# Cross attention of the first chain: values from undivided exponentials, sums by a matrix of ones, division behind the values

## The chip, the core and the metric

The kernel runs on one core of one Trainium2 chip. The metric is the device time of one execution in microseconds (us), the median of several runs. The core has a matrix engine (TensorE, PE in the profile, with PEld for its weight loads), VectorE (DVE), ScalarE (ACT), GpSimd (POOL) and the queue that issues DMAs (SP). Each engine works through its own instructions in program order and waits on semaphores for the others.

## What is computed

The reference passes x (2 x 1024 x 256, fp32) and a context of 2 x 64 rows through four layers: a decoder block (L0), a gated routing update (L1), a transformer block (L2) and a last cross attention (L3). The change touches the cross attention of L0 alone, with H = 16 heads of 16 dimensions and S = 64 context rows:

```python
q = (h @ q_w + q_b).reshape(B, T, H, HD).transpose(0, 2, 1, 3)
k = (enc @ k_w + k_b).reshape(B, S, H, HD).transpose(0, 2, 1, 3)
v = (enc @ v_w + v_b).reshape(B, S, H, HD).transpose(0, 2, 1, 3)
attn = jnp.einsum('bhtd,bhsd->bhts', q, k) * scale
attn = jnp.where(enc_mask[:, None, None, :], neg, attn)
attn = jax.nn.softmax(attn, axis=-1)
ca = jnp.einsum('bhts,bhsd->bhtd', attn, v).transpose(0, 2, 1, 3).reshape(B, T, C)
x = x + ca @ out_w + out_b
```

## The kernel before

The program is a row of parts. The one of interest is `part_chain0`, which carries everything of L0 behind its self attention, and all of L1. It takes the tokens in 4 blocks (`BLOCKS`). A block holds two streams s = 0 and 1, one for each batch entry, and a stream has two tiles t = 0 and 1 of 128 tokens. Block 0 and block 3 are written out; blocks 1 and 2 are turns of one loop (`chain_blocks`). Each stream owns four of the eight banks of PSUM, `ch.ps[s]`, 128 x 2048 fp32, and every stage of the block writes there in turn, so a stage has to be read out before the next may write.

Every engine has its order of work written out by hand in `emit`. For the cross attention of a block before:

- PE makes the scores of both streams: 1024 columns for a tile, 16 heads of 64 context rows (L1117, with the mask added by L876).
- DVE takes for each of the four pairs (s, t) in turn the maximum of each head (L987) and the difference (L989, which writes `ch.scores`). ACT takes the exponential of a pair in place (L1009). DVE sums the exponentials of a pair per head (L976) and inverts the 16 sums (L979), each pair's sums standing behind the difference of the next pair. POOL multiplies the pair's 1024 columns by the inverses (L1023).
- PE then runs `turn(0)`, `values(0)`, `turn(1)`, `projected(0)`, `values(1)`, `projected(1)`. `turn(s)` transposes 16 tiles of 128 x 128 into all four banks of the stream (L1136). `values(s)` multiplies by the values (L1143): 8 matmuls whose weights are only 32 columns wide (`e.vcol`, two heads of 16 dimensions), so that four of them stand side by side in the array; they write `ch.ps[s][:, 0:512]`. `projected(s)` multiplies by the output weights (L1152) and adds the bias (L876).
- Between `turn` and `values` the transposed tile goes to SBUF as `ch.pT[s]`: ACT copies stream 0 (L1012), DVE copies stream 1 in one instruction of 128 x 2048 (L996). Between `values` and `projected` ACT copies the result to `caT[s]` (L1342).
- Behind its copy of stream 1 DVE has `finish_block(i - 1)` in its queue, except in block 0. This is the norm n6 that closes the block before, with names in `c_t_` (L806, L811, L839, L846), and two answers of POOL that it waits for (L827, L830). Only then come, for each stream, the sum with x (L1031) and the norm n3, whose result `c_h` PE turns (L883) before the MLP begins (L1217).

A fp32 matmul stands as two rows in the trace and as one in the lists of instructions below.

Of the kernel before, what the change touches and what calls it, by code (L numbers as in the profile page):

```python
# [5 lines left out]
ALU = mybir.AluOpType  # L6
ACT = mybir.ActivationFunctionType
# [586 lines left out]
def part_context0(nc, e, A, later):  # L594
    with ExitStack() as ctx:
# [55 lines left out]
        @block.vector  # L651
        def _(dve):
            dve.memset(e.vcol[:], 0.0).then_inc(zeroed, 1)
            dve.wait_ge(w_in, ALL_W)
            for b in range(B):
                dve.tensor_scalar(e.bias0[:, b], mask8[:, b].unsqueeze(1).to_broadcast([P, 8, S2]), MASKED, None,
                                  ALU.mult)
            dve.tensor_scalar(e.q_bs[:], q_b[:], 0.25, None, ALU.mult)
            dve.wait_ge(gp.sem, gp.value("second"))
            head_rep = head16[:].unsqueeze(2).to_broadcast([P, 8, S2])  # L660
            dve.wait_ge(ev.sem, ev.value("kT"))
            for b in range(B):
                for g in range(KC):
                    rep = kT[:, g, b * S2:(b + 1) * S2].unsqueeze(1).to_broadcast([P, 8, S2])
                    dve.tensor_tensor(out=e.kbd[:, b, g].rearrange("p (h s) -> p h s", s=S2), in0=rep, in1=head_rep,
                                      op=ALU.mult)
            dve.wait_ge(zeroed, 1)
            dve.wait_ge(pe.sem, pe.value("v"))
            by_head = lambda ap: ap.rearrange("p (c e d) -> p c e d", c=8, e=2)
            for b in range(B):  # L670
                for x in range(2):
                    rows = slice(S2 * x, S2 * x + S2)
                    dve.tensor_tensor(out=e.vcol[rows, b, :, 16 * x:16 * x + 16],
                                      in0=by_head(ps["v"][rows, b * C:(b + 1) * C])[:, :, x, :],
                                      in1=by_head(v_brep[rows])[:, :, x, :], op=ALU.add)
# [57 lines left out]
def norm_steps(name):  # L733
    return [f"{name}.stats", f"{name}.moments", f"{name}.h"]
# [225 lines left out]
    return ch.scores[s][:].rearrange("p t n -> p (t n)")[:, 0:2 * cols].rearrange("p (t n) -> p t n", t=2)  # L960


def cross_vector_steps(name):
    return [f"{name}.{x}" for x in ("top0", "less0", "top1", "less1", "total0", "inverse0", "total1", "inverse1",
                                    "turned_kept")]


def cross_vector(dve, ch, name, i, cols):

    heads = cols // S2  # L970
    by_head = lambda ap: ap.rearrange("p (h k) -> p h k", k=S2)
# [11 lines left out]
    for s in range(B):  # L983
        for t in range(2):
            src, top = by_head(ch.ps[s][:, t * cols:(t + 1) * cols]), ch.top[s][:, t, 0:heads]
            after(dve, ch.te[s], f"{name}.scores{t}", i)
            dve.tensor_reduce(top, src, AX.X, ALU.max).then_inc(ch.dve[s].sem, ch.dve[s].one(f"{name}.top{t}"))  # L987
            after(dve, ch.dve[s], f"{name}.top{t}", i)
            dve.tensor_tensor(out=sc(s, t), in0=src, in1=top.unsqueeze(2).to_broadcast([P, heads, S2]),  # L989
                              op=ALU.subtract).then_inc(ch.dve[s].sem, ch.dve[s].one(f"{name}.less{t}"))  # L990
            if last:
                sums(*last)
            last = (s, t)
    sums(*last)
    after(dve, ch.te[1], f"{name}.turned", i)
    dve.tensor_copy(ch.pT[1][:, 0:cols // P, :].rearrange("p c n -> p (c n)"), ch.ps[1][:, 0:2 * cols]).then_inc(  # L996
        ch.dve[1].sem, ch.dve[1].one(f"{name}.turned_kept"))
# [67 lines left out]
def part_chain0(nc, e, A):  # L1065
    with ExitStack() as ctx:
        w = e.w0
        te_steps = ["n2.T", "ca.q", "ca.scores0", "ca.scores1", "ca.turned", "ca.v", "ca.out", "n3.T", "mlp.up", "mlp.down", "n4.T", "rt.scores",
                    "rt.turned", "rt.routed", "n5.T", "gates", "cand"]
        dve_steps = (norm_steps("n2") + cross_vector_steps("ca") + ["ca.x"] + norm_steps("n3")  # L1070
                     + ["xc"] + norm_steps("n4") + ["rt.top", "rt.minus", "rt.inverse", "rt.probs"]
                     + norm_steps("n5") + ["reset"])
        act_steps = ["n2.hT", "ca.qT", *cross_scalar_steps("ca"), "ca.vT", "n3.hT", "mlp.gelu",
                     "x.T", "n4.hT", "rt.exp", "rt.kept", "n5.hT",
                     "r", "u", "tanh"]
        ch = Chain(nc, ctx, "c0", te_steps, dve_steps, act_steps,
                   ["n2.shifted", "n2.rstd", "ca.probs0", "ca.probs1", "n3.shifted", "n3.rstd", "n4.shifted",
                    "n4.rstd", "n5.shifted", "n5.rstd"], e.biases0.shape[1])
        tail = Tail(nc, ctx, ch, "c0_tail", norm_steps("n6") + ["out.x"],
                    ["cand.less", "cand.gated", "mixed", "n6.shifted", "n6.rstd"])  # L1080
# [1 line left out]
        ROWS_MADE = 1 + 5 * (e.biases0.shape[1] // PIECE)  # L1082
        stT, inT, rT = ch.sb("stT", [P, KC, 256]), ch.sb("inT", [P, KC, 256]), ch.sb("rT", [P, KC, 256])
        qT, caT = ch.sb("qT", [P, KC, 256]), ch.sb("caT", [P, KC, 256])
        u, cand = ch.sb("u", [P, 2, C]), ch.sb("cand", [P, 2, C])
        rp, rpT = ch.sb("rp", [P, 2, P]), ch.sb("rpT", [S2, 256])
        top, total = ch.sb("rtop", [P, 2]), ch.sb("rtotal", [P, 2])
# [11 lines left out]
        def _(te):  # L1099
# [31 lines left out]
            def cross(i):  # L1131
                def turn(s):
                    for t in range(2):
                        after(te, ch.pool[s], f"ca.probs{t}", i)
                        for c in range(8):
                            ins = te.transpose(ch.ps[s][:, c * 256 + t * P:c * 256 + (t + 1) * P],  # L1136
                                               ch.scores[s][:, t, c * P:(c + 1) * P], e.ident[:])
                    ins.then_inc(ch.te[s].sem, ch.te[s].one("ca.turned"))

                def values(s):  # L1140
                    after(te, (ch.act, ch.dve)[s][s], "ca.turned_kept", i)
                    for c in range(8):
                        ins = te.matmul(ch.ps[s][32 * (c % 4):32 * (c % 4) + 32, 256 * (c // 4):256 * (c // 4 + 1)],  # L1143
                                        e.vcol[:, s, c, :], ch.pT[s][:, c, :], start=True, stop=True)
                    ins.then_inc(ch.te[s].sem, ch.te[s].one("ca.v"))

                def projected(s):
                    after(te, ch.act[s], "ca.vT", i)
                    for t in range(2):
                        dst = ch.ps[s][:, 512 + t * C:512 + (t + 1) * C]  # L1150
                        for g in range(KC):
# [111 lines left out]
        def _(dve):  # L1263
# [14 lines left out]
            def emit(i, first, last):  # L1278
                one = lambda s, name: (ch.dve[s].sem, ch.dve[s].one(name))
                x = lambda s: tokens(e, s, i)  # L1280
                if first:
                    head(0)
                    assert bias_rows(dve, ch, e.biases0, PIECE) == ROWS_MADE
                cross_vector(dve, ch, "ca", i, 1024)
                if not first:
                    finish_block(i - 1)
                for s in range(B):
# [34 lines left out]
        def _(act):  # L1322
# [13 lines left out]
            def emit(i, first, last):  # L1336
                if first:
                    head(0)
                cross_scalar(act, ch, "ca", i, 1024)
                for s in range(B):  # L1340
                    after(act, ch.te[s], "ca.v", i)
                    act.activation(caT[s][:].rearrange("p g t -> p (g t)"), ch.ps[s][:, 0:512],  # L1342
                                   ACT.Identity).then_inc(*one(s, "ca.vT"))
                for s in range(B):
                    after(act, ch.te[s], "n3.T", i)
                    turned_scalar(act, ch, s, 0, ch.hT[s], w.vec["ln3_g"], w.vec["ln3_b"]).then_inc(*one(s, "n3.hT"))
# [50 lines left out]
        def _(pool):  # L1397
# [3 lines left out]
            def emit(i, first, last):  # L1401
                if first:
                    norm_gpsimd(pool, ch, e, "n2", 0)
                cross_gpsimd(pool, ch, "ca", i, 1024)
                if not first:
                    norm_gpsimd(pool, tail, e, "n6", i - 1)
                for name in ("n3", "n4", "n5"):
# [887 lines left out]
def program(nc, A, out):  # L2295
    with ExitStack() as ctx:
# [27 lines left out]
        front = ctx.enter_context(ExitStack())  # L2324
        fb = lambda n, s, d=F32: front.enter_context(nc.sbuf_tensor(n, s, d))
        e.kbd, e.vcol = fb("kbd", [P, B, KC, 512]), fb("vcol", [P, B, 8, 32])
        e.q_w, e.q_bs, e.o_w = fb("q_w", [P, KC, C]), fb("q_bs", [P, KC]), fb("o_w", [P, KC, C])

        e.biases0 = fb("biases0", [P, 4 * C + B * 512])
# [36 lines left out]
```

## Time and profile before

| | us |
|---|---|
| median of 3 runs | 2385.2 (2384.72 to 2385.51) |
| the profiled execution | 2383.92 |
| its span, first to last instruction | 2382.2 |
| `part_chain0` in it | about 419, from 457 to 876 |
| mean granted clock of TensorE | 0.943 of full speed |

The span is what the profiler shows; the device time of the same execution is 1.7 us longer. Over the span PE is busy 88%, DVE 47%, ACT 39%, POOL 33%. Within `part_chain0` a block takes 103 to 107 us. The profile also gives the clock that the throttle granted to TensorE: 1.00 stands for 2.4 GHz and 0.50 for 1.2 GHz.

### The profile page before, as it was taken

What the parts mean: (1) busy time and instruction counts of PE and PEld (TensorE: products, weight loads), DVE (VectorE), ACT (ScalarE), POOL (GpSimd) and SP (SyncE); (2) the same over time, 40 slices, a digit from 0 to 9 for tenths busy, and PEclk for the clock granted to TensorE, in tenths of its full rate; (3) what the DMA queues carried; (4) which work ended last, traced back from release to release, by engine and by line L of the source; (5) the groups of instructions that cost most, each with busy time, mean ns of one, the idle gap of its engine ahead of it and who ended that gap; (6) DMA issues with size and microseconds to landing.
All of it is one profiled execution on the core that took longest, in us unless ns stands there. A gap on an engine that the chain in (4) does not pass through costs nothing. (4 is left out here: it accounts for less than half of the span.)

```text
span 2382.2 us, 27289 instructions
## 1 busy us (share of the span) xinstructions
PE 2086.4 (88%) x10510; PEld 1203.7 (51%) x10550; DVE 1130.7 (47%) x2031; ACT 933.0 (39%) x1435; POOL 777.5 (33%) x508
## 2 busy tenths in 40 slices
PE   2789998487979767999999999999998979898987
PEld 1444444275757554433343335334433857576766
DVE  5476672435252435455535554555450152525343
ACT  2256665133333322555545553554454422121211
POOL 3211100013032121566646664666466010202011
PEclk8899999699989887999999999999999989899989
DMA  5723320400000004000000000000000500000000
GB/s 121 130 37 44 42 29 2 113 1 0 1 0 0 1 1 122 1 1 1 1 1 1 1 1 1 1 2 1 1 2 1 161 27 1 9 1 9 0 9 9
DMA packets 48266, 52.77 MB, mean 22 GB/s; under 512 B 14730, under 2 KB 39052, under 8 KB 47732
## 3 DMA queue, kind: packets, MB, share of 16 engines
q1 hardware_dynamic: 48148, 51.17, 10.3%
q8 instruction: 77, 1.26, 0.2%
q14 instruction: 41, 0.34, 0.1%
HBM read 41.31 MB, written 8.80 MB: 21 GB/s over the span
## 5 line engine op out<-in xcount | busy, mean ns | idle before, releaser
L1731 POOL TENSOR_TENSOR total<-total,pr 128x1024 f32<-128x1024 f32 x192 | 465.1, 2423 | 241.9 <-ACT pr L1872 229.0
L1872 ACT ACTIVATE pr<-sc 128x1024 f32<-128x1024 f32 x256 | 260.0, 1022 | 355.3 <-PE sc L1651 355.3
L1752 DVE TENSOR_REDUCE pmax<-ring 128x1 f32<-128x512 f32 x512 | 325.9, 685 | 133.9 <-PE ring L1618 125.8
L1669 PE MATMUL o<-pr,v_pair 128*64 128x512 f32 x1024 | 275.7, 617 | 1.2
L1651 PE MATMUL sc<-q_full,k_full 64*128 64x512 f32 x1024 | 267.2, 591 | 0.0
L522 ACT ACTIVATE probs<-s 128x512 f32<-128x512 f32 (+1 forms) x304 | 163.2, 575 | 101.5 <-PE s L309 55.0
L1618 PE MATMUL ring<-k_round,q_round 64*128 64x512 f32 x512 | 185.0, 598 | 5.3 <-DVE pmax L1752 4.3
L1023 POOL TENSOR_TENSOR c_scores<-c_scores,c_total 128x1024 f32<-128x1024 f32 (+1 forms) x48 | 77.0, 1616 | 344.5 <-DVE c_total L979 344.5
L1618 PEld LDWEIGHTS ring<-k_round,q_round 64*128 64x128 f32 x512 | 74.4, 188 | 155.1 <-DVE pmax L1752 97.2
L394 DVE TENSOR_REDUCE row_max<-s 128x1 f32<-128x640 f32 (+3 forms) x128 | 127.3, 1020 | 47.3 <-PE s L291 47.1
L1669 PEld LDWEIGHTS o<-pr,v_pair 128*64 128x64 f32 x1024 | 51.2, 134 | 144.4 <-issue 142.6
L1731 POOL TENSOR_TENSOR total<-pr 128x1024 f32<-128x1024 f32 x32 | 75.3, 2353 | 141.8 <-ACT pr L1872 141.8
L2166 PE MATMUL c_ps<-c_hT,hT 128*128 128x256 f32 x512 | 117.3, 392 | 4.4 <-ACT c_hT L898 4.4
L288 PE MATMUL s<-k_stack,q_stack 128*128 128x512 bf16 (+3 forms) x367 | 92.9, 328 | 30.3 <-DMA k_stack<-mask_dram 16.7
L898 ACT ACTIVATE c_hT<-c_ps,c_ln_b,c_ln_g 128x256 f32<-128x256 f32 x64 | 32.4, 561 | 213.2 <-PE c_ps L883 213.2
L948 PE MATMUL c_ps<-vw,c_pT 128*128 128x256 f32 x384 | 100.0, 421 | 13.3 <-ACT c_pT L1012 13.3
L2166 PEld LDWEIGHTS c_ps<-c_hT,hT 128*128 128x128 f32 x512 | 100.2, 197 | 19.7 <-ACT c_hT L898 5.4
L1648 PE MATMUL sc<-shift,picks 64*128 64x512 bf16 x512 | 104.8, 387 | 4.8 <-DMA shift<-top_dram 4.8
L827 POOL TENSOR_TENSOR c_rstd<-c_moments,eps 128x2 f32<-128x2 f32 x48 | 9.4, 196 | 304.2 <-DVE c_moments L811 304.2
L1651 PEld LDWEIGHTS sc<-q_full,k_full 64*128 64x128 f32 x1024 | 104.6, 192 | 6.9
L306 PE MATMUL s<-q_stack,k_stack 128*128 128x512 bf16 (+3 forms) x361 | 99.3, 325 | 1.2 <-ACT probs L522 0.9
L948 PEld LDWEIGHTS c_ps<-vw,c_pT 128*128 128x128 f32 x384 | 79.8, 213 | 28.4 <-ACT c_pT L1012 15.3
(285 smaller groups left out, 3430.1 us busy)
## 6 DMA issues: line engine op xcount, KB each, us to landing
qk_dram<-qk_parts SPq DMA_DIRECT2D x32, 192.0 KB, 3.1
q_stack<-qk_dram SPq DMA_DIRECT2D x48, 128.0 KB
k_stack<-qk_dram SPq DMA_DIRECT2D x48, 128.0 KB
x<-in_x SPq DMA_DIRECT2D x4, 512.0 KB, 7.3
mlp_w<-in_L_xattn_mlp_w SPq DMA_DIRECT2D x2, 1024.0 KB, 8.1
wq<-in_L_xattn_Wq SPq DMA_DIRECT2D x2, 1024.0 KB, 6.6
wo<-in_L_xattn_Wo SPq DMA_DIRECT2D x2, 1024.0 KB, 14.9
hT<-in_L_xattn_ff_w SPq DMA_DIRECT2D x1, 2048.0 KB, 19.0
```

The costliest lines, as they stand in the source:

```text
L306: ins = te.matmul(dst[:, x * width:(x + 1) * width], k[:, j, kt * P:(kt + 1) * P], q[:, j, c0:c0 + width], start=True, stop=not diagonal)
L394: dve.tensor_reduce(row_max[:, heads[0], t:t + 1], src[:, 0:(t + 1) * P], AX.X, ALU.max).then_inc(s1_free, 1)
L522: act.activation(probs[at % KEPT][:, heads[0]:heads[-1] + 1, 0:width], s2[u % RING][:, 0:len(heads) * width].rearrange("p (j q) -> p j q", ...
L948: ins = te.matmul(dst, ch.pT[s][:, c, t * P:(t + 1) * P], vw[:, s, c, :], start=c == 0, stop=c == cols // P - 1 and out_bias is None)
L1618: te.matmul(ring[i % RING][:], qr[head[j], t * P:(t + 1) * P], kr[head[j], halves[half]], start=True, stop=True).then_inc(s1_made, 1)
L1648: te.matmul(s2[at % 2][:, j], picks[head[j]], shift[n % 2][head[j], halves[half]], start=True, stop=False)
L1651: ins = te.matmul(s2[at % 2][:, j], kf[n % 2][head[j], keys], qf[n % 2][head[j], halves[half]], start=False, stop=True)
L1669: ins = te.matmul(o[64 * j:64 * j + 64], v[n % 2][:, kt, 64 * j:64 * j + 64], probs[(U * n + u) % KEPT][:, j], start=kt == 0, stop=kt == T ...
L1731: pool.tensor_tensor(out=total[half][:], in0=other[:], in1=probs[at % KEPT][:], op=ALU.add).then_inc(sums, 1)
L1752: dve.tensor_reduce(part_max[:, j, t, half:half + 1], ring[i % RING][:], AX.X, ALU.max).then_inc(s1_free, 1)
L1872: act.activation(probs[here % KEPT][:], s2[at % 2][:], ACT.Exp).then_inc(s2_free, 1)
L2166: ins = te.matmul(ch.ps[s][:, 1024 * part + 256 * f:1024 * part + 256 * (f + 1)], w.f1[:, k, chunk * P:(chunk + 1) * P], ch.hT[s][:, k, :] ...
```

## The change

Only the cross attention of `part_chain0` changes; the two later cross attentions, which share helpers with it, keep their sums.

```diff
@@ setup, VectorE @@
             dve.memset(e.vcol[:], 0.0).then_inc(zeroed, 1)
+            dve.memset(e.sums_of[:], 0.0).then_inc(zeroed, 1)
+            dve.wait_ge(zeroed, 2)
+            for x in range(2):
+                dve.memset(e.sums_of[S2 * x:S2 * x + S2, 16 * x:16 * x + 16], 1.0)
...
-            dve.wait_ge(zeroed, 1)
@@ cross_vector @@
-            if last:
+            if last and sums_made:
                 sums(*last)
             last = (s, t)
-    sums(*last)
+    if sums_made:
+        sums(*last)
@@ part_chain0, TensorE, cross @@
                     for t in range(2):
-                        after(te, ch.pool[s], f"ca.probs{t}", i)
+                        after(te, ch.dve[s], "ca.less1", i)
+                        after(te, ch.act[s], f"ca.exp{t}", i)
...
                         ins = te.matmul(ch.ps[s][32 * (c % 4):32 * (c % 4) + 32, 256 * (c // 4):256 * (c // 4 + 1)],
                                         e.vcol[:, s, c, :], ch.pT[s][:, c, :], start=True, stop=True)
+                    for c in range(8):
+                        ins = te.matmul(ch.ps[s][32 * (c % 4):32 * (c % 4) + 32, 1024 + 256 * (c // 4):1280 + 256 * (c // 4)],
+                                        e.sums_of[:], ch.pT[s][:, c, :], start=True, stop=True)
                     ins.then_inc(ch.te[s].sem, ch.te[s].one("ca.v"))
 
                 def projected(s):
-                    after(te, ch.act[s], "ca.vT", i)
+                    after(te, ch.dve[s], "ca.vT", i)
@@ part_chain0, VectorE, emit @@
-                cross_vector(dve, ch, "ca", i, 1024)
+                cross_vector(dve, ch, "ca", i, 1024, sums_made=False)
+                for s in range(B):
+                    after(dve, ch.te[s], "ca.v", i)
+                    dve.reciprocal(inverse[s][:], ch.ps[s][:, 1024:1536]).then_inc(*one(s, "ca.inverse"))
+                    after(dve, ch.dve[s], "ca.inverse", i)
+                    dve.tensor_tensor(out=caT[s][:].rearrange("p g t -> p (g t)"), in0=ch.ps[s][:, 0:512],
+                                      in1=inverse[s][:], op=ALU.mult).then_inc(*one(s, "ca.vT"))
                 if not first:
                     finish_block(i - 1)
@@ part_chain0, ScalarE, emit @@
-                for s in range(B):
-                    after(act, ch.te[s], "ca.v", i)
-                    act.activation(caT[s][:].rearrange("p g t -> p (g t)"), ch.ps[s][:, 0:512],
-                                   ACT.Identity).then_inc(*one(s, "ca.vT"))
@@ part_chain0, GpSimd, emit @@
-                cross_gpsimd(pool, ch, "ca", i, 1024)
```

`e.sums_of` is a 128 x 32 matrix with ones where a row and a column belong to the same head of a pair. A matmul with it gives the sum of the head's exponentials, 16 times over, at the places where the values of that head lie; so the division is one by one between two 128 x 512 arrays.

Two places in the order of instructions of block 3, the written out one (blocks 0 to 2 have the same order). First TensorE, from the transposes of stream 0 to the first projection of stream 1, before:

```order
L1136 MATMUL c0_ps0<-ident,c0_scores0 128x128 x16
L1143 MATMUL c0_ps0<-c0_pT0,vcol 32x256 x8
L1136 MATMUL c0_ps1<-ident,c0_scores1 128x128 x16
L1152 MATMUL c0_ps0<-o_w,c0_caT0 128x256 x2
L876 MATMUL c0_ps0<-c0_rows,c0_ones 128x256
L1152 MATMUL c0_ps0<-o_w,c0_caT0 128x256 x2
L876 MATMUL c0_ps0<-c0_rows,c0_ones 128x256
L1143 MATMUL c0_ps1<-c0_pT1,vcol 32x256 x8
L1152 MATMUL c0_ps1<-o_w,c0_caT1 128x256 x2
```

and with the change, where lines are numbered a little higher:

```order
L1145 MATMUL c0_ps0<-ident,c0_scores0 128x128 x16
L1152 MATMUL c0_ps0<-c0_pT0,vcol 32x256 x8
L1156 MATMUL c0_ps0<-c0_pT0,sums_of 32x256 x8
L1145 MATMUL c0_ps1<-ident,c0_scores1 128x128 x16
L1165 MATMUL c0_ps0<-o_w,c0_caT0 128x256 x2
L879 MATMUL c0_ps0<-c0_rows,c0_ones 128x256
L1165 MATMUL c0_ps0<-o_w,c0_caT0 128x256 x2
L879 MATMUL c0_ps0<-c0_rows,c0_ones 128x256
L1152 MATMUL c0_ps1<-c0_pT1,vcol 32x256 x8
L1156 MATMUL c0_ps1<-c0_pT1,sums_of 32x256 x8
L1165 MATMUL c0_ps1<-o_w,c0_caT1 128x256 x2
```

The groups keep their order; eight matmuls with `sums_of` have come behind each stream's values.

Then VectorE with the change, from the last difference of the cross attention to the start of `finish_block` (names in `c0_t_`). Before, L996 stood directly ahead of the rows of `finish_block`:

```order
L994 TENSOR_TENSOR c0_scores1<-c0_ps1,c0_top1 128x1024
L1002 COPY c0_pT1<-c0_ps1 128x2048
L1300 RECIPROCAL c0_inverse0<-c0_ps0 128x512
L1302 TENSOR_TENSOR c0_caT0<-c0_ps0,c0_inverse0 128x512
L1300 RECIPROCAL c0_inverse1<-c0_ps1 128x512
L1302 TENSOR_TENSOR c0_caT1<-c0_ps1,c0_inverse1 128x512
L794 MEMSET c0_t_spare0 1x1
L809 BN_STATS c0_t_stats0<-c0_xc0 128x6 x2
```

The two divisions stand between the copy of stream 1 and `finish_block`, and both streams' `caT` come from this queue.

## Rows read from the trace of the kernel before

**Rows 1.** Busy time, `part_chain0`: stretch, length, five engines with counts, clock, DMA

```profile
457.00:876.00 419.00, 352.34 (x1700) 271.38 (x1698) 172.43 (x414) 137.62 (x275) 87.82 (x109) 0.91 0.00 1
```

**Rows 2.** Timeline, block 1, softmax: start, length, engine, line, work [idle before it]

```profile
564.86 1.23 DVE L987 TENSOR_REDUCE c_top<-c_ps 128x16 f32<-128x1024 f32 x1 [6.79 <-PE c_ps L876]
566.12 1.23 DVE L989 TENSOR_TENSOR c_scores<-c_ps,c_top 128x1024 f32<-128x1024 f32 x1
...
568.51 1.23 DVE L989 TENSOR_TENSOR c_scores<-c_ps,c_top 128x1024 f32<-128x1024 f32 x1
...
570.91 0.38 PE L876 MATMUL c_ps<-c_rows,c_ones 96*128 96x512 bf16 x1
...
577.27 1.06 ACT L1009 ACTIVATE c_scores<-c_scores 128x1024 f32<-128x1024 f32 x1 [2.69 <-DVE c_scores L989]
...
578.73 3.76 POOL L1023 TENSOR_TENSOR c_scores<-c_scores,c_total 128x1024 f32<-128x1024 f32 x2 [1.85 <-DVE c_total L979]
578.94 1.94 ACT L1012 ACTIVATE c_pT<-c_ps 128x1024 f32<-128x1024 f32 x2 [0.61 <-PE c_ps L1136]
```

**Rows 3.** Timeline of block 1, values and projections, and what follows

```profile
580.93 1.93 PE L1143 MATMUL c_ps<-c_pT,vcol 128*32 128x256 f32 x16 [2.03 <-ACT c_pT L1012]
...
582.80 2.44 PE L1136 MATMUL c_ps<-ident,c_scores 128*128 128x128 f32 x16
...
584.96 0.73 PEld L1152 LDWEIGHTS c_ps<-o_w,c_caT 128*128 128x128 f32 x4
...
585.27 2.29 DVE L996 COPY c_pT<-c_ps 128x2048 f32<-128x2048 f32 x1 [5.25 <-PE c_ps L1136]
...
586.91 0.27 PE L876 MATMUL c_ps<-c_rows,c_ones 96*128 96x256 bf16 x1
587.49 0.42 DVE L806 BATCH_NORM_STATS2 c_t_stats<-c_xc 128x6 f32<-128x256 f32 x1
...
587.62 1.07 PE L1143 MATMUL c_ps<-c_pT,vcol 128*32 128x256 f32 x16 [0.43 <-DVE c_pT L996]
...
593.63 0.69 DVE L1031 TENSOR_TENSOR x<-c_ps,x 128x512 f32 x1
...
597.27 1.11 PE L883 MATMUL c_ps<-ident,c_h 128*128 128x128 f32 x4 [5.65 <-DVE c_h L818]
...
599.50 6.07 PE L1217 MATMUL c_ps<-c_hT,mlp_w 128*128 128x256 f32 x16 [1.11 <-ACT c_hT L898]
```

**Rows 4.** VectorE's groups by shape, whole program: count, busy us, mean ns, idle before

```profile
L979 DVE RECIPROCAL c_total<-c_total 128x16 f32<-128x16 f32 x32 | 8.1, 253 | 1.1
...
L979 DVE RECIPROCAL c_total<-c_total 128x8 f32<-128x8 f32 x16 | 3.3, 203 | 0.6
...
L1302 DVE RECIPROCAL c_rtotal<-c_rtotal 128x2 f32<-128x2 f32 x8 | 1.3, 166 | 6.1 <-ACT c_rp L1363 6.1
```

**Rows 5.** Busy time by stretches of 4 us, columns as in rows 1

```profile
573.00:577.00 4.00, 1.71 (x9) 1.31 (x10) 3.93 (x5) 1.06 (x1) 2.03 (x2) 0.57 0.00 0
...
581.00:585.00 4.00, 4.00 (x32) 2.73 (x33) 0.00 (x0) 0.60 (x1) 1.49 (x1) 0.65 0.00 0
...
593.00:597.00 4.00, 0.00 (x0) 0.00 (x0) 2.83 (x11) 0.00 (x0) 0.89 (x2) 0.63 0.00 0
...
601.00:605.00 4.00, 4.00 (x13) 3.23 (x12) 0.00 (x0) 0.00 (x0) 0.00 (x0) 0.59 0.00 0
...
705.00:709.00 4.00, 4.00 (x10) 3.19 (x11) 0.74 (x2) 0.00 (x0) 0.35 (x1) 0.50 0.00 0
...
713.00:717.00 4.00, 4.00 (x20) 3.54 (x19) 0.00 (x0) 2.87 (x7) 0.00 (x0) 1.00 0.00 0
```

**Rows 6.** Timeline of block 0: start of the softmax, sum with x, turning of n3

```profile
467.77 1.23 DVE L987 TENSOR_REDUCE c_top<-c_ps 128x16 f32<-128x1024 f32 x1 [0.70 <-PE c_ps L876]
...
491.13 0.68 DVE L1031 TENSOR_TENSOR x<-c_ps,x 128x512 f32<-128x512 f32 x1
...
495.11 0.60 PE L883 MATMUL c_ps<-ident,c_h 128*128 128x128 f32 x4
```

More of the change, by code:

```diff
@@ L960, in scores_of, with cross_vector_steps, cross_vector @@
     return ch.scores[s][:].rearrange("p t n -> p (t n)")[:, 0:2 * cols].rearrange("p (t n) -> p t n", t=2)
-def cross_vector_steps(name):
+def cross_vector_steps(name, sums=True):
+    if not sums:
+        return [f"{name}.{x}" for x in ("top0", "less0", "top1", "less1", "turned_kept")]
     return [f"{name}.{x}" for x in ("top0", "less0", "top1", "less1", "total0", "inverse0", "total1", "inverse1",
                                     "turned_kept")]
-def cross_vector(dve, ch, name, i, cols):
+def cross_vector(dve, ch, name, i, cols, sums_made=True):
     heads = cols // S2
@@ L1069, in part_chain0 @@
                     "rt.turned", "rt.routed", "n5.T", "gates", "cand"]
-        dve_steps = (norm_steps("n2") + cross_vector_steps("ca") + ["ca.x"] + norm_steps("n3")
+        dve_steps = (norm_steps("n2") + cross_vector_steps("ca", False) + ["ca.inverse", "ca.vT", "ca.x"] + norm_steps("n3")
                      + ["xc"] + norm_steps("n4") + ["rt.top", "rt.minus", "rt.inverse", "rt.probs"]
                      + norm_steps("n5") + ["reset"])
-        act_steps = ["n2.hT", "ca.qT", *cross_scalar_steps("ca"), "ca.vT", "n3.hT", "mlp.gelu",
+        act_steps = ["n2.hT", "ca.qT", *cross_scalar_steps("ca"), "n3.hT", "mlp.gelu",
                      "x.T", "n4.hT", "rt.exp", "rt.kept", "n5.hT",
@@ L1076, in part_chain0 @@
         ch = Chain(nc, ctx, "c0", te_steps, dve_steps, act_steps,
-                   ["n2.shifted", "n2.rstd", "ca.probs0", "ca.probs1", "n3.shifted", "n3.rstd", "n4.shifted",
+                   ["n2.shifted", "n2.rstd", "n3.shifted", "n3.rstd", "n4.shifted",
                     "n4.rstd", "n5.shifted", "n5.rstd"], e.biases0.shape[1])
@@ L1084, in part_chain0 @@
         qT, caT = ch.sb("qT", [P, KC, 256]), ch.sb("caT", [P, KC, 256])
+        inverse = ch.sb("inverse", [P, 512])
         u, cand = ch.sb("u", [P, 2, C]), ch.sb("cand", [P, 2, C])
@@ L2326, in program @@
         e.kbd, e.vcol = fb("kbd", [P, B, KC, 512]), fb("vcol", [P, B, 8, 32])
+        e.sums_of = fb("sums_of", [P, 32])
         e.q_w, e.q_bs, e.o_w = fb("q_w", [P, KC, C]), fb("q_bs", [P, KC]), fb("o_w", [P, KC, C])
```

## The prediction

> **What bounds the kernel now.** I read the busy shares of the page first: PE is busy 88% of the span, so time is lost where PE stands still or runs at the low clock. The stretches then show that the chain which is changed takes 419 us and that PE is busy in 352 of them [rows 1]. The timeline of one block shows where the other 67 us lie: in each of the four blocks PE waits during the softmax of the cross attention, and again between the last projection and the turning of n3. So the cross attention is a path of dependent steps on several engines, not work that PE covers, and a step moved on that path counts in full.
>
> The path of block 1. DVE starts at 564.86 and goes through maximum, difference, sums and reciprocal of four pairs. The last exponential starts at 577.27, POOL's last two products end at 582.49, while ACT copies the transposed stream 0 from 578.94 to 580.88 [rows 2]. PE makes values(0) from 580.93 and turn(1) from 582.80 to 585.24; DVE copies stream 1, and has this behind it at 587.49, when `finish_block` starts; that takes 6.14 us, up to the sum with x at 593.63 [rows 3]. Everything later (norm n3, its turning at 597.27, the MLP) hangs on this sum. So what decides in blocks 1 to 3 is **when DVE reaches `finish_block`**: at 587.49. Projection(0) and values(1) run beside the copy and beside `finish_block`, and cost nothing now; nor does ACT's copy of `caT`. In block 0, which has no `finish_block`, the sum follows the copy at once (491.13) and the end is PE's second projection, behind which n3 is turned at 495.11 [rows 6].
>
> **What is removed.** Sixteen sums and sixteen small reciprocals (0.25 us each [rows 4]) leave DVE, sixteen products leave POOL. Differences of two pairs then follow each other at 2.39 us, as the first two do now (566.12 and 568.51); PE has all scores ready by 571.29, before the fourth pair's 572.0 [rows 2]. The fourth difference starts at 566.12 + 3 x 2.39 = 573.29, and the last exponential runs from 574.55 to 575.6. Turn(0) runs from 571.3 to about 573.7, and ACT's copy, queued behind the last exponential, from 575.6 to 577.55: 3.3 us earlier than 580.88. That is the whole gain on the path at this point. POOL's 3.76 us for two products lay beside that copy and beside values(0), so removing them only frees turn(1).
>
> **What is added on PE.** Eight more matmuls of the form of values behind each stream's values. Values(0), at the low clock, hands over to turn(1) after 1.87 us (580.93 to 582.80), of which 1.72 us are passes; values(1), at the high clock, takes 1.07 us [rows 3], of which 0.86 are passes. The sums add these passes again: 1.72 us low, 0.86 us high. The clock matters, and rows 5 show it by stretches. PE's last work before the pause ended at 571.29, and the stretch 573 to 577 has a mean of 0.57 (full until about 573.6, then half); behind the end at 591.6 the stretch 593 to 597 has 0.63 (half from about 594.0). It came back at about 583.8 (0.65 in 581 to 585) after PE had begun values(0) at 580.93, at about 604.3 (0.59 in 601 to 605) after the MLP had begun at 599.5 [rows 3]; and in block 2 not within 705 to 709, all of it dense work (0.50). In the changed block PE pauses from 573.7 to 577.6, 3.9 us, so I take values(0) and its sums at the low clock: 577.6 + 1.87 + 1.72 = 581.2. Turn(1) took 2.44 us with the clock rising within; risen a little before its start, I take 2.2, ends 583.4. The copy's start to its successor's start is 2.22 us: **DVE is free at 585.6**, 1.9 us earlier than now.
>
> **What is added on DVE.** Per stream one reciprocal of 128 x 512 and one product of 128 x 512, both on the path: `projected(0)` waits for the first pair, `values(1)` stands behind `projected(0)` in PE's queue, the second pair waits for `values(1)`, and `finish_block` stands behind the second pair in DVE's queue. None of this has cover. The product is of the form of the sum with x, 0.69 us [rows 3], with its wait 0.75. No reciprocal of 512 columns is in the trace, but three sizes are: 2 columns 166 ns, 8 columns 203 ns, 16 columns 253 ns [rows 4]. That is (203 - 166) / 6 = 6.2 and (253 - 203) / 8 = 6.25 ns for each further column, a straight line: 154 + 512 x 6.2 = 3330 ns, and some 60 ns for reading PSUM, so **3.4 us**. The nearest long rows would bound it from below: DVE's copy of 2048 columns in 2.29 us is 1.12 ns a column, 0.57 us for 512. I take 3.4, because the line goes through three rows of this very instruction while the copy is another one.
>
> These rows show 6.2 ns a column for the reciprocal. The Trainium skill (page "VectorE: DVE Perf Modes", section "First, the fixed hardware budget") says that a reciprocal is an iterative division with a repeat count of 8; at that page's engine clock of 0.96 GHz eight cycles would be an estimate of 8.3 ns a column, 4.4 us. The rows agree that it iterates, not on the size; by the page the sum below would be 8 x 1.0 = 8 us longer.
>
> **The sum for a block.** From 585.6: reciprocal 3.4, product 0.75, PE at 589.8. PE has been idle for 6.4 us, so the projection runs at the low clock: now it takes 2.2 us (584.96 to 587.18 [rows 3]), and since 10 matmuls fit into 4 us at the low clock and 20 at the high one [rows 5], 4.1 us: 593.9. Values(1) and sums at the high clock, 1.07 + 0.86 and the handing over, 2.0 us: 595.9. Second reciprocal and product 4.15: **600.05**. Whether the clock is back by 593.9, 4.1 us after PE resumed, is open: of the times above one says yes (2.9 us) and two say later (4.8 and over 4); I add 0.4 us. So `finish_block` starts at 600.45 in place of 587.49: **+13.0 us** in blocks 1, 2 and 3, 39.0 together. The second projection, 4.1 us at the low clock, runs beside the 6.14 us of `finish_block`. If that cover were gone, it would be on the path as in block 0.
>
> In block 0 the start is 467.77 in place of 564.86, so the second product ends at 600.45 - 97.09 = 503.4. PE's second projection, at the low clock behind another pause of 4 us, ends at 507.5; n3(0), which now takes 3.6 us from the sum with x, is ready at 507.0. The turning starts at 507.5 and not at 495.11 [rows 6]: **+12.4 us**.
>
> Edits that cost nothing: three small memsets in the setup, while DVE waits for weights; ACT's copy of `caT` gone, which was no longer than what replaces it; POOL freed, on which only the small norms wait. Behind the sum with x nothing is changed, and the MLP begins behind a pause of about 5.6 us as now, at the low clock as now. Sum: 39.0 + 12.4 = 51.4. Against the profiled execution 2383.9 + 51.4 = 2435.3; the median of the runs stands 1.3 above it: 2436.6, so **2436 us**.
>
> **The rivals.**
>
> 1. The clock stays high throughout the cross attention. For it: pauses of 4 us are short; against it: it fell after pauses of about 2.3 and 2.4 us in rows 5. Values(0) with sums would end at 579.5, turn(1) at 581.7, the copy at 583.9, first division 588.05, projection 590.3, values 592.3, second division 596.45: +8.95 a block, and in block 0 n3(0) is ready at 499.4 + 3.6 = 503.0, +7.85. Together 34.7: 2420 us.
> 2. The clock stays low through values(1): 1.93 for 1.07 and 1.72 for 0.86, less the 0.4 already taken, about +1.3 in four blocks, and up to 2 us in the MLP of block 0, which now starts soon after dense work: 2444 us.
> 3. The division needs eight cycles a column: 8 reciprocals x 1.0 us more, 2445 us. Against it stand three sizes on one line of 6.2 ns. It is the page's rule named above.
> 4. The division streams like a copy, 0.57 us in place of 3.4. Eight of them save 22.6 us: 2414 us. For it only the copy's row, against it rows 4: 16 columns would then take about 16 ns more than 2 columns, not 87.
> 5. The other side, not slower: the long reciprocal streams and thereby shortens the pauses so that PE keeps the high clock, through the start of the MLP too, where the low clock from 599.5 to 604.3 costs half of these 4.8 us, 2.4 in each of blocks 1 to 3. Then 34.7 - 3 x 2.4 - 8 x 2.83 = 4.9 us: 2390, at the edge of no change. It decides from a reciprocal of 0.56 us downward; since even a reciprocal of no length leaves two products and a projection in the queue ahead of `finish_block`, a real gain hardly exists.
>
> **How the numbers follow.** Forecast 0.70, its own range 2426 to 2442; rival 1 0.12; rival 2 0.07; rival 3 0.05; rival 4 0.04; rival 5 0.02. The range 2420 to 2448 takes in rivals 1 to 3 and the sizes between. About 0.2% (4.8 us) is what a measurement of this kernel can tell from no change. Only rival 5 ends there, half of it and some unforeseen gain below: faster 0.01, same 0.02, slower 0.97.
>
> **What would show it.** In the profile after: a group of 8 reciprocals of 128 x 512 with a mean near 3.4 us (rival 3: 4.4; rival 4: 0.6); PE's first projection of block 1 beginning some 25 us after the first maximum (now 20.1) and taking about 4 us; `finish_block` starting 35.6 us after the first maximum, where it is 22.6 now; two idle times of DVE for `ca.v`, the second about 6 us; blocks of 116 to 118 us in place of 103 to 107; the rest of the program the same length. The clock by stretches decides between the forecast and rivals 1 and 2. Wrong would be the whole argument if `finish_block` did not start behind the second product, or if the blocks grew by less than the two divisions.

## The result and the profile after

| | us |
|---|---|
| before, median of 4 runs | 2385.11 (2384.72 to 2385.51) |
| with the change, median of 4 runs | 2433.61 (2431.83 to 2437.14) |
| ratio | 1.0205, 95% interval 1.0192 to 1.0217 |
| profiled execution: span before, after | 2382.2, 2431.3 |

The change makes the kernel 48 us slower. The forecast was 2436 us, in a range of 2420 to 2448.

Line numbers of the changed kernel are higher by 3 to 19 in this part. The page of the changed kernel: engine, busy us, share of the span, instructions.

```profile
span 2431.3 us, 27503 instructions
PE 2103.2 (87%) x10638; PEld 1210.4 (50%) x10678; DVE 1141.5 (47%) x2018; ACT 927.1 (38%) x1427; POOL 746.4 (31%) x492
```

POOL lost 31 us of work (16 products) and PE gained 17; neither moved the end by its own length. `part_chain0` is told from its timeline: from the first maximum of block 0 to the first statistics of the next part. In the changed kernel the marks are these (start, length, engine, line, work, idle time before it and what ended it):

```profile
469.68 1.23 DVE L992 TENSOR_REDUCE c_top<-c_ps 128x16 f32<-128x1024 f32 x1 [0.70 <-PE c_ps L879]
...
579.44 1.23 DVE L992 TENSOR_REDUCE c_top<-c_ps 128x16 f32<-128x1024 f32 x1 [6.79 <-PE c_ps L879]
...
696.22 1.22 DVE L992 TENSOR_REDUCE c_top<-c_ps 128x16 f32<-128x1024 f32 x1 [6.80 <-PE c_ps L879]
...
812.21 1.23 DVE L992 TENSOR_REDUCE c_top<-c_ps 128x16 f32<-128x1024 f32 x1 [6.79 <-PE c_ps L879]
...
933.50 5.33 DVE L1461 BATCH_NORM_STATS2 stats_all<-x 128x6 f32<-128x256 f32 x16 [0.33 <-PEq L1072]
```

That is 463.8 us; the same stretch before was 418.7, from 467.77 [rows 6] to this row of the kernel before:

```profile
886.50 5.32 DVE L1447 BATCH_NORM_STATS2 stats_all<-x 128x6 f32<-128x256 f32 x16 [0.33 <-PEq L1066]
```

Counted from first maximum to first maximum, blocks 0 to 3 took 97.1, 105.0, 105.6 and 111.0 us before (the text ahead of the prediction says 103 to 107) and take 109.8, 116.8, 116.0 and 121.3 now. 45.1 of the span's 49.1 us are made there, +12.7, +11.8, +10.4 and +10.3 in blocks 0 to 3. The other 4.0 lie outside, where nothing was changed: the chain begins 1.9 us later, and what follows it is 2.1 longer. The run e7 below has the same setup and begins its chain at 467.63, so the new memsets are not the cause. Over the eleven kernels profiled here the time outside the chain runs from 1962.6 us (e9) to 1969.6 (e4), and single executions of the kernel before differed by as much (2383.2 to 2389.4 us in the comparisons below).

Block 1 of the changed kernel, the rows that answer to rows 2 and 3:

```profile
589.13 1.06 ACT L1015 ACTIVATE c_scores<-c_scores 128x1024 f32<-128x1024 f32 x1 [1.33 <-DVE c_scores L994]
590.09 1.92 ACT L1018 ACTIVATE c_pT<-c_ps 128x1024 f32<-128x1024 f32 x2
...
592.06 1.93 PE L1152 MATMUL c_ps<-c_pT,vcol 128*32 128x256 f32 x16 [4.44 <-ACT c_pT L1018]
...
593.77 1.87 PE L1156 MATMUL c_ps<-c_pT,sums_of 128*32 128x256 f32 x16
...
595.57 1.97 PE L1145 MATMUL c_ps<-ident,c_scores 128*128 128x128 f32 x16
597.58 2.29 DVE L1002 COPY c_pT<-c_ps 128x2048 f32<-128x2048 f32 x1 [8.48 <-PE c_ps L1145]
599.78 3.35 DVE L1300 RECIPROCAL c_inverse<-c_ps 128x512 f32<-128x512 f32 x1
603.17 0.69 DVE L1302 TENSOR_TENSOR c_caT<-c_ps,c_inverse 128x512 f32<-128x512 f32 x1
...
603.91 2.08 PE L1165 MATMUL c_ps<-o_w,c_caT 128*128 128x256 f32 x4 [6.37 <-DVE c_caT L1302]
...
608.05 1.56 PE L1152 MATMUL c_ps<-c_pT,vcol 128*32 128x256 f32 x16
...
609.44 1.04 PE L1156 MATMUL c_ps<-c_pT,sums_of 128*32 128x256 f32 x16
610.55 3.36 DVE L1300 RECIPROCAL c_inverse<-c_ps 128x512 f32<-128x512 f32 x1 [6.70 <-PE c_ps L1156]
613.95 0.69 DVE L1302 TENSOR_TENSOR c_caT<-c_ps,c_inverse 128x512 f32<-128x512 f32 x1
614.56 0.42 DVE L809 BATCH_NORM_STATS2 c_t_stats<-c_xc 128x6 f32<-128x256 f32 x1
...
620.71 0.68 DVE L1037 TENSOR_TENSOR x<-c_ps,x 128x512 f32 x1
```

Read it as a relay: reciprocal, product, projection (603.91 to 608.1), values and sums (608.05 to 610.5), reciprocal, product, and only then `finish_block` at 614.56, 35.1 us after the block's first maximum; it was 22.6. VectorE stands idle twice, 8.48 us before the copy and 6.70 us before the second reciprocal, and works on the path in between. The group of the reciprocals (count, busy us, mean ns, idle before them and what ended it):

```profile
L1300 DVE RECIPROCAL c_inverse<-c_ps 128x512 f32<-128x512 f32 x8 | 26.8, 3353 | 26.6 <-PE c_ps L1156 26.6
```

The clock around this path (stretch, length, busy us of PE, PEld, DVE, ACT, POOL with counts, granted clock, DMA share, GB/s):

```profile
589.00:593.00 4.00, 0.94 (x12) 0.48 (x16) 0.09 (x1) 2.88 (x3) 0.00 (x0) 0.88 0.00 0
593.00:597.00 4.00, 4.00 (x41) 2.33 (x34) 0.00 (x0) 0.00 (x0) 0.00 (x0) 0.69 0.02 4
597.00:601.00 4.00, 0.54 (x5) 0.30 (x3) 3.42 (x2) 0.00 (x0) 0.00 (x0) 1.00 0.00 0
601.00:605.00 4.00, 1.09 (x3) 0.91 (x4) 2.82 (x2) 0.00 (x0) 0.00 (x0) 0.66 0.00 0
605.00:609.00 4.00, 4.00 (x21) 2.29 (x23) 0.00 (x0) 0.00 (x0) 0.00 (x0) 0.50 0.00 0
609.00:613.00 4.00, 1.48 (x28) 0.58 (x20) 2.45 (x1) 0.00 (x0) 0.00 (x0) 0.93 0.00 0
```

It went down to 1.2 GHz at the end of the pause before the values of stream 0 (about 592.0) and again in the pause behind turn(1) (about 602.3), and the first projection ran at 1.2 GHz from end to end. In blocks 2 and 3 it rose during the sums of stream 0 already; block 2 (1.87 us in block 1):

```profile
710.55 1.51 PE L1156 MATMUL c_ps<-c_pT,sums_of 128*32 128x256 f32 x16
```

### The profile page after: what moved, and what is told of

Same layout as the page of the kernel before. It is cut to its first block and busy times, and to the rows that moved or that the text cites. A ratio compares the mean times of both kernels' runs of the same rounds, so it can differ in the third digit from the quotient of the medians.

```text
span 2431.3 us, 27503 instructions
## 1 busy us (share of the span) xinstructions
PE 2103.2 (87%) x10638; PEld 1210.4 (50%) x10678; DVE 1141.5 (47%) x2018; ACT 927.1 (38%) x1427; POOL 746.4 (31%) x492
## 5 line engine op out<-in xcount | busy, mean ns | idle before, releaser
L1745 POOL TENSOR_TENSOR total<-total,pr 128x1024 f32<-128x1024 f32 x192 | 464.7, 2420 | 242.0 <-ACT pr L1886 229.1
L901 ACT ACTIVATE c_hT<-c_ps,c_ln_b,c_ln_g 128x256 f32<-128x256 f32 x64 | 32.4, 560 | 307.8 <-PE c_ps L886 307.8
L1029 POOL TENSOR_TENSOR c_scores<-c_scores,c_total 128x1024 f32<-128x1024 f32 (+1 forms) x32 | 46.7, 1471 | 287.7 <-DVE c_total L984 287.7
```

The source lines that it names most:

```text
L1745: pool.tensor_tensor(out=total[half][:], in0=other[:], in1=probs[at % KEPT][:], op=ALU.add).then_inc(sums, 1)
```

## The experiments

Each experiment was timed beside the kernel before, on the same chip. Beside its median stands the length of the chain in its profiled execution, measured between the two marks above; this leaves out what varies elsewhere.

| kernel | median us | ratio to before (95%) | chain us |
|---|---|---|---|
| before | 2385.1 | | 418.7 |
| with the change | 2433.6 | 1.0205 (1.0192 to 1.0217) | 463.8 |
| e1 copy for reciprocal | 2416.8 | 1.0124 (1.0106 to 1.0141) | 446.2 |
| e2 finish_block early | 2409.0 | 1.0098 (1.0081 to 1.0115) | 443.0 |
| e3 values(1) first | 2408.0 | 1.0092 (1.0075 to 1.0109) | 440.3 |
| e4 TensorE kept busy | 2424.2 | 1.0159 (1.0142 to 1.0176) | 455.9 |
| e5 sums twice | 2440.3 | 1.0229 (1.0212 to 1.0246) | 472.5 |
| e6 before, finish_block early | 2366.4 | 0.9912 (0.9895 to 0.9930) | 399.6 |
| e7 division by ScalarE | 2410.8 | 1.0114 (1.0097 to 1.0132) | 443.5 |
| e8 short path | 2367.1 | 0.9926 (0.9909 to 0.9942) | 399.6 |
| e9 both orders | 2380.6 | 0.9982 (0.9972 to 0.9992) | 415.5 |

My theory was the sum of the prediction: long reciprocals, a projection and values between them, and `finish_block` behind all of it, each in full on the path, with a tensor clock that falls in the pauses. The rivals were that one or another of these is covered.

### e1: the length of the reciprocal

```diff
-                    dve.reciprocal(inverse[s][:], ch.ps[s][:, 1024:1536]).then_inc(*one(s, "ca.inverse"))
+                    dve.tensor_copy(inverse[s][:], ch.ps[s][:, 1024:1536]).then_inc(*one(s, "ca.inverse"))
```

> The changed kernel, with the eight long reciprocals replaced by copies of the same 128 x 512 from PSUM, so the values are multiplied by the sums and not divided by them. Theory (the length of the reciprocal on the path is most of the cost): the copy takes about 0.6 us where the reciprocal took 3.35, 8 x 2.75 = 22 us less than the changed kernel's 2433.6: 2412 us, and down to 2404 if the shorter pauses keep the tensor clock up. Rival (the added dependency links cost, not the division's length): at most 8 us less, 2426 or more.

Measured 2416.8 us, 16.8 less than the changed kernel, and a chain 17.6 shorter. The rival (at most 8) is out. The gain is short of the 22 expected for two reasons. The copy took more than I took from the long one:

```profile
L1300 DVE COPY c_inverse<-c_ps x8: 680/686/692, 490.4 to 826.2; 128x512 f32<-128x512 f32 x8
```

(shortest, median and longest in ns), so 8 x (3.35 - 0.69) = 21.3. In blocks 2 and 3 `finish_block` and the MLP then came 4.8 us earlier within the block (the MLP at 41.7 us behind the first maximum, not 46.6), but the block was only 3.4 shorter: the rest went in the MLP. So the reciprocal's length is worth 17 to 21 us, under half of the 45.

### e2: finish_block out of the way

```diff
@@ cross_vector, ahead of the copy L1002 @@
+    between()
     after(dve, ch.te[1], f"{name}.turned", i)
@@ emit, VectorE @@
-                cross_vector(dve, ch, "ca", i, 1024, sums_made=False)
+                cross_vector(dve, ch, "ca", i, 1024, sums_made=False,
+                             between=lambda: first or finish_block(i - 1))
...
-                if not first:
-                    finish_block(i - 1)
```

> The changed kernel, with finish_block(i - 1) moved on VectorE from behind the divisions to ahead of the copy of stream 1, where VectorE stands idle for 8.1 to 8.5 us. Theory (finish_block behind the second product is on the path, and its 6.1 us fit into that idle time): the copy starts when it did, the sum with x follows the second product at once, and the turning of n3 then waits for the second projection; 5.5 us less in each of three blocks, 16.5 together, 2417 us, and up to 7 less still if the MLP then begins at the high clock: 2410. Rival (finish_block is covered by the second projection anyway): no more than 4 us less.

Measured 2409.0 us, 24.6 less (chain 20.8 shorter), a little past the better end of what was expected. In blocks 1 to 3 the MLP begins 5.2 to 5.8 us earlier and the blocks are 6.6 to 7.3 us shorter, so some 1.4 us a block were gained behind the MLP's start. The timeline of block 1 shows both halves of it: `finish_block` fits into the idle time, and the copy still waits for TensorE; the sum with x follows the second product at once.

```profile
588.84 0.42 DVE L809 BATCH_NORM_STATS2 c_t_stats<-c_xc 128x6 f32<-128x256 f32 x1
...
593.40 1.67 DVE L849 SCALAR_TENSOR_TENSOR x<-c_t_h,c_t_rstd,r_o_b 128x256 f32 x4
...
597.40 2.29 DVE L1003 COPY c_pT<-c_ps 128x2048 f32<-128x2048 f32 x1 [2.33 <-PE c_ps L1146]
...
613.78 0.69 DVE L1304 TENSOR_TENSOR c_caT<-c_ps,c_inverse 128x512 f32<-128x512 f32 x1
614.38 0.68 DVE L1038 TENSOR_TENSOR x<-c_ps,x 128x512 f32 x1
```

### e3: values(1) ahead of projected(0)

```diff
-                projected(0)
                 values(1)
+                projected(0)
                 projected(1)
```

> The changed kernel, with values(1) ahead of projected(0) in TensorE's order. Theory (the first projection and the second values stand on the path only because of TensorE's order, between the two divisions): the second reciprocal starts right behind the first product, 6.6 us earlier, in all four blocks: 26 us less, 2407 us. Rival (VectorE's two divisions alone set the pace): unchanged within 4 us.

Measured 2408.0 us, 25.6 less (chain 23.5 shorter). The values and sums of stream 1 run beside the first reciprocal, the second reciprocal follows the first product without a gap, and the projection runs beside it:

```profile
594.10 3.35 DVE L1300 RECIPROCAL c_inverse<-c_ps 128x512 f32<-128x512 f32 x1
594.24 1.07 PE L1152 MATMUL c_ps<-c_pT,vcol 128*32 128x256 f32 x16 [2.38 <-DVE c_pT L1002]
...
598.09 3.35 DVE L1300 RECIPROCAL c_inverse<-c_ps 128x512 f32<-128x512 f32 x1
598.23 1.13 PE L1165 MATMUL c_ps<-o_w,c_caT 128*128 128x256 f32 x4 [2.06 <-DVE c_caT L1302]
```

So TensorE's order, not its work, put 6.7 us a block between the two divisions.

### e4: the clock

```diff
                 turn(1)
+                spent(0, 12)
                 projected(0)
                 values(1)
+                spent(0, 8)
                 projected(1)
```

Here `spent(s, n)` issues n matmuls of 128 x 256 into `ch.ps[s][:, 1536:1792]`.

> The changed kernel, with TensorE fed in both of its pauses: 12 matmuls of 128 x 256 behind turn(1) and 8 behind values(1), into a bank that nobody reads. Their results are not used. Theory (the pauses let the clock fall, and the projection of stream 0 and the values of stream 1 pay for it on the path): the projection takes 2.2 us in place of 4.1, values and sums 2.0 in place of 2.4 to 2.8; about 2.4 us a block and 2 more in block 0, 12 us less, 2422 us. Rival (the clock is no matter here, or the added matmuls are late themselves): within 3 us or slower.

Measured 2424.2 us, 9.4 less (chain 7.9 shorter). The clock stayed up through both divisions of block 1, and the projection, from 601.73 on, was done by 603.9, in 2.2 us where the changed kernel needed 4.2:

```profile
598.00:602.00 4.00, 2.81 (x13) 2.17 (x12) 3.64 (x2) 0.00 (x0) 0.00 (x0) 1.00 0.00 0
602.00:606.00 4.00, 4.00 (x43) 2.48 (x43) 0.12 (x1) 0.00 (x0) 0.00 (x0) 1.00 0.00 0
606.00:610.00 4.00, 3.46 (x16) 2.70 (x15) 3.97 (x4) 0.00 (x0) 0.00 (x0) 1.00 0.00 0
```

The low clock that these two pauses bring therefore costs 8 us of the chain's 45 (9.4 of the 48 by the medians). The pause before values(0) was left as it is, and its share was not tried, although the banks of stream 1 lie free there from the last difference on.

### e5: the sums on TensorE

```diff
-                    for c in range(8):
+                    for c in list(range(8)) * 2:
                         ins = te.matmul(ch.ps[s][32 * (c % 4):32 * (c % 4) + 32, 1024 + 256 * (c // 4):1280 + 256 * (c // 4)],
                                         e.sums_of[:], ch.pT[s][:, c, :], start=True, stop=True)
```

> The changed kernel, with the eight matmuls by the matrix of ones issued twice for each stream; the result is the same. Theory (the sums on TensorE are on the path in both streams): 1.72 us at the low clock in stream 0 and 0.86 at the high one in stream 1, less what an earlier return of the clock gives back: 4 to 10 us more than the changed kernel's 2433.6, 2438 to 2444. Rival (they are hidden, by VectorE's copy for instance): within 2 us.

Measured 2440.3 us, 6.7 more (chain 8.7 longer), within the expected 4 to 10. One more set made blocks 0 to 3 longer by 0.4, 1.8, 3.1 and 3.4 us, about 2 us on average. In the changed kernel the one set thus costs some 7 to 9 us in all; this is argued from doubling, not shown by leaving it out.

### e6: the same move in the kernel before

```diff
-                cross_vector(dve, ch, "ca", i, 1024)
-                if not first:
-                    finish_block(i - 1)
+                cross_vector(dve, ch, "ca", i, 1024, between=lambda: first or finish_block(i - 1))
```

> The kernel before the change, with finish_block(i - 1) moved ahead of VectorE's copy of stream 1 in the same way. There VectorE is idle for 5.3 us and finish_block takes 6.1, so the copy comes 0.9 us later, but the sum with x is ready at once and n3 is turned when the second projection ends, some 4.8 us earlier in three blocks, with up to 2.4 us each for an MLP at the high clock. Theory (the cost of the change on a common footing is its own, and the order of finish_block was a cost of both kernels): 14 to 21 us less than before, 2364 to 2371 us; the change then costs about 40 us against it. Rival (finish_block hurts only behind the long divisions): within 4 us of before.

Measured 2366.4 us, ratio 0.9912: 19 us faster than before. The move of e2, made in the kernel before, is worth nearly as much there. Block 1 shows what limits it. VectorE has no room for the whole of `finish_block`, the copy comes at 587.20 without a wait (1.7 us later in the block than before, where 0.9 was expected), and n3 is turned when the second projection is done:

```profile
587.20 2.28 DVE L997 COPY c_pT<-c_ps 128x2048 f32<-128x2048 f32 x1
...
594.92 0.60 PE L883 MATMUL c_ps<-ident,c_h 128*128 128x128 f32 x4
```

The first maximum of this block is at 565.14, so n3 is turned 29.8 us behind it, where rows 2 and 3 give 32.4. Since both kernels gain by this move, it does not explain their difference; it is a cost that both had. With the move in both, e2 against e6, the change still costs 42.7 us (43.4 by the chain).

### e7: the division by ScalarE

```diff
-                    dve.reciprocal(inverse[s][:], ch.ps[s][:, 1024:1536]).then_inc(*one(s, "ca.inverse"))
...
+                    act.activation(inverse[s][:], ch.ps[s][:, 1024:1536], ACT.Ln).then_inc(*one(s, "ca.log"))
+                    after(act, ch.act[s], "ca.log", i)
+                    act.activation(inverse[s][:], inverse[s][:], ACT.Exp, scale=-1.0).then_inc(*one(s, "ca.inverse"))
```

> The changed kernel, with the reciprocal made by ScalarE, which is idle there: the logarithm of the sums from PSUM, then the exponential of its negative; VectorE only multiplies. Orders are otherwise as in the changed kernel. Theory (a reciprocal of 3.35 us replaced by two steps of 0.6 us and a wait, about 1.3 us, and for stream 0 beside VectorE's copy): 3.4 + 2.1 us less a block, 22 together, and up to 8 more by the clock: 2404 to 2412 us. Rival (tables have to be exchanged, 1.28 us each way): nothing gained over the changed kernel, or less than 8 us.

Measured 2410.8 us, 22.8 less (chain 20.3 shorter). The size fits the theory, but its rival was half right: tables are exchanged between the logarithm and the exponential, for both streams.

```profile
587.32 0.60 ACT L1359 ACTIVATE c_inverse<-c_ps 128x512 f32<-128x512 f32 x1 [2.15 <-PE c_ps L1156]
587.93 1.28 ACT L1361 ACT_TABLE_LOAD   x1
589.23 0.63 ACT L1361 ACTIVATE c_inverse<-c_inverse 128x512 f32<-128x512 f32 x1
589.87 1.28 ACT L1359 ACT_TABLE_LOAD   x1
```

From the logarithm's start to the exponential's end are 2.54 us in place of the 1.3 expected and the reciprocal's 3.35. By these rows stream 1 gains 0.8 us a block. In block 1, where `finish_block` begins 7.0 us earlier than in the changed kernel, 3.7 us are stream 0's, whose division lies beside VectorE's copy now. Another 2.5 lie between the first projection and the logarithm of stream 1: that stretch takes 4.1 us (592.12 to 596.27) where the changed kernel takes 6.6, since the first projection runs at the high clock there and takes 2.2 us and not 4.1. Blocks 0 and 3 show this too; in block 2 the projection takes 4.1 us, and `finish_block` begins only 3.2 us earlier.

### e8: a short path with undivided exponentials

The division of e7, and the moves that its expectation lists. On VectorE:

```diff
+                def between():
+                    if not first:
+                        finish_block(i - 1)
+                    divided(0)
...
                 for s in range(B):
+                    if s:
+                        divided(s)
                     add_vector(dve, ch, e, "ca.x", i, "ca.out", s, bank=1)
```

> The division by logarithm and exponential on ScalarE, with four moves: finish_block and the first product ahead of VectorE's copy of stream 1, the sum with x and norm n3 of stream 0 ahead of the second product, and the turning of n3 of stream 0 ahead of the second projection. Theory (undivided exponentials do shorten the path by what POOL's products and the sums took, once no division and no finish_block stands on it): the MLP begins 26.9 us after the first maximum; before the change it begins 34.6 us after it in blocks 1 to 3 and 29.0 in block 0, so 8 us less a block in three and 2 in one: 26 us less than before, 2359 us, with the clock 2352. Rival (the gain of e6 is all there is, and undivided exponentials bring nothing further): 2366 to 2372 us. Second rival (the extra links eat it): 2380 or more.

Measured 2367.1 us, ratio 0.9926: faster than before, but level with e6 in median and chain (399.6 both). The expected 2359 was missed. The MLP of block 1 begins 30.5 us behind the first maximum (566.66), not 26.9:

```profile
590.33 0.60 ACT L1366 ACTIVATE c_inverse<-c_ps 128x512 f32<-128x512 f32 x1 [3.68 <-PE c_ps L1157]
...
590.94 1.28 ACT L1368 ACT_TABLE_LOAD   x1
...
593.65 2.08 PE L1166 MATMUL c_ps<-o_w,c_caT 128*128 128x256 f32 x4 [0.85 <-DVE c_caT L1300]
...
597.13 3.62 PE L1231 MATMUL c_ps<-c_hT,mlp_w 128*128 128x256 f32 x16
```

The second division had the exchange of tables in it, and the MLP, which I had counted from n3 of stream 0, stands behind the second projection in TensorE's queue, and that took 3.5 us. So the rival of the expectation holds: the gain of e6 is all there is, and undivided exponentials bring nothing further in this form.

### e9: the changed kernel's instructions in another order

The moves of e2 and e3 together; on top of e2's diff:

```diff
-                projected(0)
                 values(1)
+                projected(0)
                 projected(1)
```

> The changed kernel with both moves of order, finish_block ahead of the copy and values(1) ahead of projected(0); its instructions are those of the changed kernel. Theory (the change costs what it does mostly because its division stands ahead of finish_block and on both sides of a projection; with both moved, the MLP begins 34.5 us after the first maximum of a block, where it is 34.6 in the kernel before and 46.8 in the changed one): 17 us less than with values(1) ahead alone (2408), and up to 6 more by the clock, 2385 to 2391, level with the kernel before, and 19 to 25 above the kernel before with its finish_block moved (2366). Rival (the two moves give back the same time, so they don't add): 2400 or more.

Measured 2380.6 us, ratio 0.9982: 53 us less than the changed kernel, with the same instructions. The two moves gave 24.6 and 25.6 alone; they add up (by the chain 20.8 and 23.5, and 48.3 together). In block 1 one division follows the other and the sum with x follows them:

```profile
591.11 3.35 DVE L1302 RECIPROCAL c_inverse<-c_ps 128x512 f32<-128x512 f32 x1
...
595.10 3.35 DVE L1302 RECIPROCAL c_inverse<-c_ps 128x512 f32<-128x512 f32 x1
...
598.48 0.69 DVE L1304 TENSOR_TENSOR c_caT<-c_ps,c_inverse 128x512 f32<-128x512 f32 x1
599.09 0.68 DVE L1038 TENSOR_TENSOR x<-c_ps,x 128x512 f32 x1
...
604.49 3.72 PE L1231 MATMUL c_ps<-c_hT,mlp_w 128*128 128x256 f32 x16 [1.11 <-ACT c_hT L901]
```

The MLP begins 33.5 us behind the first maximum (570.97), 1.0 earlier than the expected 34.5, and at the high clock; in the other blocks it is 33.5 to 34.2. Four blocks of this make up most of the 4 us by which the time fell below the expected range. It remains 14 us above e6, which has the old way of dividing and one of the two moves. The other move, values(1) ahead of projected(0), was not tried in the kernel before, so 14 us is what remains against the best order tried there.

## Why the prediction was right, step by step

Times of block 1 are counted from its first maximum; expected ones are those of the prediction less 564.86.

| step | expected | measured |
|---|---|---|
| VectorE's copy begins | 18.5 | 18.1 (17.8 in blocks 2 and 3) |
| reciprocal of 512 columns | 3.4 | 3.35 |
| first projection begins | 24.9 | 24.5 |
| first projection lasts | 4.1 | 4.2 |
| `finish_block` begins | 35.6 | 35.1 (34.6, 34.6) |
| its shift in blocks 1, 2, 3 | +13.0 each | +12.5, +11.6, +11.5 |
| turning of n3(0) in block 0, shift | +12.4 | +12.3 |
| chain | +51.4 | +45.1 |

The mechanism held in its long links: e1 shows the reciprocal on the path, e2 `finish_block`, e3 what lies between the two divisions, e4 the clock, e5 the sums. What they give back overlaps, since a step is shortened by one and hidden by another, so the gains don't add up to the 45 us of the chain. The line through three short reciprocals gave the long one to within 2%: 3.33 us by the line and 3.35 measured. For the 60 ns added for reading PSUM no run has a row of its own; the 3.35 leave some 20 of them. The estimate that I worked out from the Trainium skill's repeat count of 8 (page "VectorE: DVE Perf Modes", section "First, the fixed hardware budget"), 4.4 us, was not borne out: the profile has 3.353 us, 6.25 ns for each column beyond the 16 of rows 4.

Some terms were sized a little wrong. The copy came 0.4 us earlier than summed in block 1, and 0.7 in blocks 2 and 3, where the clock rose during the sums of stream 0. The second reciprocal with its product took 4.0 us and not 4.15. The forecast carried block 1 over to blocks 2 and 3, but there `finish_block` had begun at 23.0 and 23.1 us before the change, not at 22.6. The 0.4 us for a late return of the clock was needed: from the first projection to the second reciprocal passed 6.6 us in block 1 and 6.5 in blocks 2 and 3, where the sum had 6.1 without it. And "behind the sum with x nothing is changed" did not quite hold: in blocks 1 to 3 the MLP began 12.5, 11.6 and 11.5 us later but the blocks grew by 11.8, 10.4 and 10.3 only, so the MLP gave back about 1 us each. Together this makes the chain 6.3 us shorter than forecast; 4.0 us that appeared outside it brought the total back to within 2.4 us of the forecast. The last closeness is therefore partly luck.

The removal was read a little wrong too, though its sum, 3.3 us, was right: ScalarE's copy of stream 0 began 3.4 us earlier in the block. The prediction puts all of it down to VectorE's sums and says that POOL's removal only frees turn(1). But in the kernel before the second half of turn(0) waited for a product of POOL, and ScalarE then stood idle for 0.61 us ahead of its copy, waiting for turn(0) [rows 2]:

```profile
576.94 1.97 PE L1136 MATMUL c_ps<-ident,c_scores 128*128 128x128 f32 x8 [2.11 <-POOL c_scores L1023]
```

So some 0.6 of the 3.4 us were POOL's. Its removal was not tried alone.

One sign did not come. The prediction names two idle times of VectorE for `ca.v`; there is one in a block, before the second reciprocal (26.6 us in four blocks). The first reciprocal follows the copy without a wait, as the sum of the prediction itself has it. Of the blocks, which were to take 116 to 118 us, blocks 1 and 2 do.

Rival 1 (clock high throughout) is refuted by the clock rows of the changed kernel; e4 prices two of its three pauses. In block 1 the clock fell 4.4 and 4.7 us after TensorE's last work, not after 2.3 and 2.4 as the prediction read rows 5; before the change it fell at 573.6 with turn(0) already running again. Rival 2 (clock low through values(1)) was half of what came in block 1: the values ran mostly at the low clock (1.56 us against 1.07), the sums at the high one (1.04). Rival 3 (eight cycles a column) is refuted by the 3353 ns. So is rival 4 (a streaming division); e1 shows what it would have given, 2417 us, near its 2414, and with it rival 5 falls. What I did not see is how much of the cost was order: I named the idle time of VectorE only as the wait in front of the copy, and not as a place for `finish_block`, which was worth 19 us to the kernel before as well.

## What to carry to other kernels

An operation that leaves a busy stage is worth only what the path gains at the next hand-over, here 3.4 us a block at ScalarE's copy, of which 2.3 to 3.1 were left at VectorE's; an operation put behind a stage counts in full, with everything that stands behind it in its engine's queue. Before a step is moved, look at both queues for work that could fill the waits it makes: the same instructions took 2434 us in one order and 2381 in another. And work in compact form where an instruction is slow per column: a reciprocal of 16 columns costs 0.25 us, one of 512 columns, in which every sum stands 16 times, 3.35.

## What the hardware showed that was not expected

A logarithm and an exponential next to each other on ScalarE brought a table exchange between them each time, 1.28 us, 16 in e7's chain; the two functions themselves took 0.60 and 0.63 us. A copy of 128 x 512 from PSUM took 0.69 us, more than a quarter of the 2.29 us for 128 x 2048. The tensor clock came back at about 609.6 (0.93 in the stretch 609 to 613), 5.7 us after TensorE had resumed with the first projection of block 1, where rows 5 gave 2.9 and 4.8 us at other places. The forecast asked whether it would be back when that projection ended, 4.1 us after its start; it was not.
